# Value products of an attention round issued one round later, in four chained layers on one core

## The reference

```
L0  x = latent attention over (ctx, x), then RMS norm, MLP 512 -> 2048 -> 512 with gelu, residual
L1  x = grouped-query attention of x over ctx (32 query heads, 8 key heads, mask added), layer norm
L2  x = cross attention of layernorm(x) over ctx (16 heads), residual, layer norm, MLP, residual
L3  x = latent attention over (ctx, x), norm, MLP, residual (as L0, other weights)
attention: softmax(scale * Q K^T + mask) V, then an output product with its bias
```

## Time and profile before

| what | value |
|---|---|
| median of 3 runs | 2698.76 us (2697.95 to 2700.19) |
| profiled execution, its own time | 2698.54 us |
| its span (first to last instruction) | 2696.8 us |
| PE / PEld / DVE busy | 2478.5 / 2080.7 / 1284.3 us |
| ACT / POOL busy | 1090.2 / 1104.4 us |
| mean granted TensorE clock | 0.966 |

### The profile page before, as it was taken

The page is one execution under the profiler, slowest core; times in us unless marked ns, Lnnn a source line. Parts: engine busy times, 40 slices in busy tenths (PEclk is TensorE's granted clock), DMA queues, the critical chain, the costliest instruction groups (busy, mean ns, idle before and its releaser), DMA issues.

```text
span 2696.8 us, 47930 instructions
## 1 busy us (share of the span) xinstructions
PE 2478.5 (92%) x18464; PEld 2080.7 (77%) x18464; DVE 1284.3 (48%) x2527; ACT 1090.2 (40%) x3705; POOL 1104.4 (41%) x1972
## 2 busy tenths in 40 slices
PE   7999998999997777758888899999899999899999
PEld 6887886888886666647777788888788888688887
DVE  4556554323226878764445533322355555432322
ACT  4555553111117777755555411111355555311111
POOL 2444446400135888973454570003345444540000
PEclk9999999999998999879989899999999999899999
DMA  4112213111122222221232241101211211321100
GB/s 154 56 56 89 70 36 106 62 45 47 59 74 70 78 91 77 66 69 61 84 103 89 73 125 48 47 34 61 83 48 48 87 48 34 105 63 47 48 32 16
DMA packets 110321, 181.25 MB, mean 67 GB/s; under 512 B 7889, under 2 KB 43409, under 8 KB 109073
## 3 DMA queue, kind: packets, MB, share of 16 engines
q1 hardware_dynamic: 110096, 178.19, 20.2%
HBM read 132.02 MB, written 46.14 MB: 66 GB/s over the span
## 4 chain that ended last, share of the span: by engine, by line
PE 78%; DVE 8%; ACT 5%; POOL 5%; issue 3%; DMA 1%; SPq 0%; DVEq 0%; POOLq 0%; ACTq 0%
PE banks L317 70%; PE banks L453 4%; ACT plain_high L697 3%; PE banks L480 3%; POOL plain_high L1268 2%; DVE neg_max L948 2%; DVE plain_high L944 2%; PE banks L504 1%; DVE plain_work L953 1%; DVE rounded_work L1046 1%; DVE rounded_work L1020 0%; DVE stats L1072 0%; DMA plain_work<-mlp_w 0%; POOL rounded_high L308 0%; PE banks L442 0%
## 5 line engine op out<-in xcount | busy, mean ns | idle before, releaser
L317 PE MATMUL banks<-rounded_work,rounded_low 128*128 128x512 f32 (+1 forms) x2688 | 533.1, 356 | 57.9 <-issue 35.3
L1268 POOL TENSOR_SCALAR plain_high<-plain_high,inv_sum 128x128 f32<-128x128 f32 (+1 forms) x1024 | 388.1, 402 | 407.7 <-DVE inv_sum L966 407.2
L317 PEld LDWEIGHTS banks<-rounded_work,rounded_low 128*128 128x128 f32 x2688 | 445.7, 200 | 124.7 <-issue 53.8
L317 PE MATMUL banks<-rounded_work,rounded_high 128*128 128x512 f32 (+1 forms) x2400 | 488.2, 358 | 8.7 <-DMA rounded_work<-ctx_split 6.2
L925 ACT ACTIVATE plain_work<-banks,columns 128x512 f32<-128x512 f32 x192 | 132.5, 690 | 865.3 <-PE banks L317 865.3
L317 PEld LDWEIGHTS banks<-rounded_work,rounded_high 128*128 128x128 f32 x2400 | 399.7, 193 | 76.4 <-issue 9.8
L1244 DVE CAST rounded_work<-plain_work 128x512 fp32r<-128x512 f32 x192 | 101.3, 528 | 693.7 <-ACT plain_work L925 682.8
L317 PE MATMUL banks<-rounded_low,rounded_work 128*128 128x512 f32 x1728 | 413.1, 391 | 0.0
L317 PE MATMUL banks<-rounded_high,rounded_work 128*128 128x512 f32 (+1 forms) x1728 | 392.8, 380 | 0.0
L317 PEld LDWEIGHTS banks<-rounded_low,rounded_work 128*128 128x128 f32 x1728 | 322.3, 188 | 68.8 <-issue 3.0
L317 PEld LDWEIGHTS banks<-rounded_high,rounded_work 128*128 128x128 f32 x1728 | 311.8, 190 | 60.4 <-issue 1.4
(11 more groups left out here) (101 smaller groups left out, 3063.4 us busy)
## 6 DMA issues: line engine op xcount, KB each, us to landing
plain_work<-x SPq DMA_DIRECT2D x96, 256.0 KB, 2.9
plain_work<-mlp_w SPq DMA_DIRECT2D x96, 256.0 KB, 2.7
rounded_work<-ctx_split SPq DMA_DIRECT2D x24, 1024.0 KB, 6.0
u<-plain_work SPq DMA_DIRECT2D x48, 256.0 KB, 2.8
plain_work<-u SPq DMA_DIRECT2D x12, 1024.0 KB, 6.7
x<-plain_work SPq DMA_DIRECT2D x48, 256.0 KB, 2.1
plain_work<-attention_w SPq DMA_DIRECT2D x44, 256.0 KB, 2.7
plain_work<-inputs_t SPq DMA_DIRECT2D x8, 1024.0 KB, 8.1
```

The costliest lines, as they stand in the source:

```text
L317: mm = pe.matmul(dst, lhs(i), rhs(j), start=first and n == 0, stop=last and n == 2, skip_group_check=True)
L1268: last = pool.tensor_scalar(part, part, inv_sum[:, R % 2, r, g:g + 1], 1.0, ALU.mult, ALU.mult)
```

## The change

The value product of round n moves behind the scores of round n+2 and ahead of the turning of round n+1, on TensorE. On ScalarE its split (`act_heads`) moves to just before the copy of row 0 of round n+1. On VectorE its split (`dve_heads`) moves into `dve_round`, behind the maxima of rows 0 and 1. The last round of a pair crosses into the next pair, and the last one of a layer stands alone after the loop. Of the diff, the latent layer on TensorE, the same in the cross layer, the helper and its use:

```
@@ pe_latent
                 pe_scores(pe, y, p, 1)
+                if p:
+                    pe_attend(pe, y, p - 1, 3)
                 pe_turn_probs(pe, y, p, 0)
...
-                pe_attend(pe, y, p, 0)
                 if more:
                     pe_keys(pe, y, p + 1, 0)
                     pe_keys(pe, y, p + 1, 1)
                 pe_scores(pe, y, p, 2)
+                pe_attend(pe, y, p, 0)
                 pe_turn_probs(pe, y, p, 1)
...
-                pe_attend(pe, y, p, 1)
...
                 pe_scores(pe, y, p, 3)
+                pe_attend(pe, y, p, 1)
                 pe_turn_probs(pe, y, p, 2)
...
-                pe_attend(pe, y, p, 2)
                 if more:
                     pe_keys(pe, y, p + 1, 3)
                     pe_scores(pe, y, p + 1, 0)
+                pe_attend(pe, y, p, 2)
                 pe_turn_probs(pe, y, p, 3)
                 pe_out(pe, y, 2 * p)
-                pe_attend(pe, y, p, 3)
...
+            pe_attend(pe, y, PAIRS - 1, 3)
             pe_out(pe, y, B - 1)
@@ pe_cross
                 pe_scores(pe, y, p, 1)
+                if p:
+                    pe_attend(pe, y, p - 1, 1)
                 pe_turn_probs(pe, y, p, 0)
                 if more:
                     pe_turn_x(pe, y, p + 1)
-                pe_attend(pe, y, p, 0)
...
                 if more:
                     pe_scores(pe, y, p + 1, 0)
+                pe_attend(pe, y, p, 0)
                 pe_turn_probs(pe, y, p, 1)
                 pe_out(pe, y, 2 * p)
-                pe_attend(pe, y, p, 1)
@@ act_cross (act_latent and act_gqa alike, with 3 for 1)
+                if p:
+                    act_heads(act, y, p - 1, 1)
                 act_round(act, y, p, 1, (p, 0), inputs)
-                act_heads(act, y, p, 0)
...
+                act_heads(act, y, p, 0)
                 act_round(act, y, p + 1, 0 if more else None, (p, 1), nothing)
-                act_heads(act, y, p, 1)
@@ dve_round
-        def dve_round(dve, y, p, k, turned, between):
+        def dve_round(dve, y, p, k, turned, between, past=None):
             if k is not None:
                 dve_max(dve, y, p, k, 0)
                 dve_max(dve, y, p, k, 1)
+            if past:
+                dve_heads(dve, y, *past)
             if turned:
                 dve_probs(dve, y, *turned, 1)
@@ dve_cross (dve_latent and dve_gqa alike)
-                dve_round(dve, y, p, 1, (p, 0), inputs)
-                dve_heads(dve, y, p, 0)
+                dve_round(dve, y, p, 1, (p, 0), inputs, (p - 1, 1) if p else None)
...
-                dve_round(dve, y, p + 1, 0 if more else None, (p, 1), nothing)
+                dve_round(dve, y, p + 1, 0 if more else None, (p, 1), nothing, (p, 0))
                 dve_out(dve, y, 2 * p)
-                dve_heads(dve, y, p, 1)
```

More of the change, by code:

```diff
@@ L1128, in dve_latent @@
                     dve_keys(dve, y, p + 1, 1)
-                dve_round(dve, y, p, 2, (p, 1), nothing)
+                dve_round(dve, y, p, 2, (p, 1), nothing, (p, 0))
                 if more:
@@ L1138, in dve_latent @@
                     dve_values(dve, y, p + 1, 1)
-                dve_round(dve, y, p, 3, (p, 2), nothing)
+                dve_round(dve, y, p, 3, (p, 2), nothing, (p, 1))
                 if more:
@@ L1144, in dve_latent @@
                     dve_turn_u(dve, M[y.n], 0, 3)
-                dve_heads(dve, y, p, 2)
                 if more:
                     dve_keys(dve, y, p + 1, 3)
-                dve_round(dve, y, p + 1, 0 if more else None, (p, 3), nothing)
+                dve_round(dve, y, p + 1, 0 if more else None, (p, 3), nothing, (p, 2))
                 dve_out(dve, y, 2 * p)
-                dve_heads(dve, y, p, 3)
                 if more:
                     dve_queries(dve, y, p + 1, 1)
+            dve_heads(dve, y, PAIRS - 1, 3)
             dve_out(dve, y, B - 1)
@@ L1223, in dve_cross @@
                     dve_out(dve, y, 2 * p - 1)
-                dve_round(dve, y, p + 1, 0 if more else None, (p, 1), nothing)
+                dve_round(dve, y, p + 1, 0 if more else None, (p, 1), nothing, (p, 0))
                 dve_out(dve, y, 2 * p)
-                dve_heads(dve, y, p, 1)
+            dve_heads(dve, y, PAIRS - 1, 1)
             dve_out(dve, y, B - 1)
```

56 lines of the change are left out of this document (32 added, 24 removed).

## The result

The moved order is slower: 2733.4 us median (2727.35 to 2737.85) beside 2698.36 (2692.72 to 2700.19) for the kernel before on the same chip, ratio 1.0134 with a 95% interval of 1.0117 to 1.0151, or +35 us. The forecast was +22.7 (2721), the range reached to 2744. The profiled execution of after took 2737.85 us with a span of 2736.0, so the two profiled spans differ by 39.2 us.

The account below looks back on a forecast made before the run. TensorE was taken as nearly full in L3 and L0, with idle time in the cross and grouped-query layers. Terms 7.4 + 2.1 + 10.5 + 7.7 + 1.0 - 6 = +22.7 us on 2698.54 gave 2721, range 2697 to 2744.

Parts of the forecast that it names:

- Cross layer, first and second round: Cross layer: keys 1.75 us later in six pairs (+10.5), row 3 of the second turning waits 1.1 in seven (+7.7).
- the shift: L0, first round: softmax and input split 1.06 us later, keys' wait 1.27 becomes 2.33, seven pairs: +7.4 us.
- rival C: L0: longer waits before the keys lower the clock there too, 22 us more, 2743; chance 0.14.
- one of the signs that I had named for being wrong: Three signs: grouped-query pair under 43 us, latent first copy less than 0.5 us later, or L0 clock below 1.00.
- 1.6 us of a pair: Grouped-query layer: 1.9 less 0.3 us off a pair's 47.45, -11 us over seven pairs, half taken off for the clock.
- waits for GpSimd take the place of those before the value product: Grouped-query layer: waits before the value product vanish, waits for POOL replace them, a pair at 46 to 47 us.
- the ring of four banks: Row 3 of the turning needs the value product's bank, free after VectorE's heads split: +7.7 us cross layer, 0 in L3.
- 0: L3 apart from its last pair: the 1.06 us shift is hidden by TensorE's own work, 0 us.
- Last pairs and the MLP's first rows: Last pairs, where TensorE waits for DMA of the MLP's rows: +1.1 us each in L0 and L3; cross layer +1.0.
- rival A: Grouped-query layer runs free once VectorE stops waiting for the value product: 5 us a pair (-35), 2692; chance 0.11.
- B: L0 and cross layer: only places change, the later softmax is swallowed and the ring does not bind: 2698.5; chance 0.09.
- the 6 us that the grouped-query layer was to give back: Grouped-query layer: scores no longer wait for the value product, net -6 us after half is taken off for the clock.

Follow-up runs that it names:

- e5_after_wide: e4_fix with each round's heads split in the grouped-query and cross layers as one instruction per engine, other biases left out: 2715.35 us, 1.0054 of before.
- e2_cross: The kernel before with the change in the cross layer alone: 2716.42 us, 1.0050 of before.
- e4_fix: The changed kernel with VectorE's last heads split of the grouped-query layer moved ahead of block 14's second moments: 2725.20 us, 1.0088 of before.
- e1_gqa: The kernel before with the change in the grouped-query layer alone, VectorE's last heads split ahead of block 14's second moments: 2699.24 us, 0.9988 of before.
- e7_gqa_norm: e1_gqa with one normalising instruction of GpSimd per row instead of four, three sums left out: 2690.27 us, 0.9967 of before.
- e8_before_ring: The kernel before with three of VectorE's four moments blocks a pair in the grouped-query layer moved ahead of the reciprocals: 2726.91 us, 1.0088 of before.
- e3_latent: The kernel before with the change in L0 and L3 alone: 2710.68 us, 1.0029 of before.
- e11_gqa_ring: e1_gqa with three of VectorE's moments blocks a pair moved ahead of the round's reciprocals: 2708.13 us, 1.0026 of before.
- e9_latent_early: e3_latent with L0's split of the next pair's inputs one step earlier on ScalarE and VectorE: 2696.83 us, 0.9979 of before.

## Why the prediction held, and where it didn't

**Cross layer, first and second round: right, mechanism and size.** +18.2 forecast, +16.0 measured, with the two waits at 5.09 and 0.96 us: the first round came out at 1.49 us a pair (1.75 forecast), the second at 0.96 (1.1). e5_after_wide takes away the split's length and with it 1.3 of the 2.3 us a pair. In after the second pair takes 45.42 us, with matmuls at a granted clock of 0.50 behind its wait of 5.80 us (1260 to 1265 us); in e2_cross and e4_fix it takes 42.07 and 42.44 after 5.57 and 5.56 us, so this part belongs to one execution.

**L0: the shift was right, the clock was not in the sum.** The copy starts 1.71 us after the step that stands first, where it was 0.70: 1.01 later (1.06 forecast). The wait of six pairs' keys grew by 0.85, and the keys of pair 1 start 0.40 us later (55.57 for 55.17): 5.5 of the 7.4. Two of six pairs pay 1.6 us more for the clock. That is rival C, in part: 3.2 us of its 22, and one of the signs that I had named for being wrong, a clock below 1.00 in L0, came (0.99). The two lines at 109.86 and 161.81 have the same wait, and the burst of matmuls behind it was fast in one pair and slow in the other.
The Trainium skill (TensorE: Matmul & The Clock Gate, "HAM oscillation — how this bites in real kernels") tells of a kernel in which the burst behind every wait starts at the low clock; the slow pair agrees with that, the fast one doesn't.

**Grouped-query layer: the step "1.6 us of a pair" failed.** Five pairs, from the third to the last input turning, give 47.06 us each in before and 46.92 in e1_gqa. I had written that waits for GpSimd take the place of those before the value product; it was the heads' split (42.6 us), and the waits for GpSimd fell from 19.9 to 16.9. I had used the ring of four banks for the cross layer and L3, not here, where the value product's bank is also the one that row 3 of the turning takes. Two cuts at single links gave little: neither a shorter split (e5_after_wide, 0.33 us) nor less normalising (e7_gqa_norm, 0.19) moved the mean of six pairs by much, though the last pair of e7_gqa_norm is 3 us shorter. What the pair's 47 us are made of stays open, with two accounts left. By one, exponentials, reciprocals, normalising, sums and maxima follow one another over four engines and hold the pair at its length whatever TensorE waits for; e8_before_ring shows of it only that late reciprocals lengthen the pair. By the other, the gain came and the clock took it: 1.2 us more of matmuls a pair at 0.87 for 0.91, beside the 1.6 us that the pair was to lose, of which the prediction had taken off half. No run has the new order in this layer at the old clock, so the runs don't tell the two apart.

**The end of the grouped-query layer: missing from the sum.** The edit moved VectorE's last heads' split behind the moments of block 14, which wait for GpSimd. The prediction counted the last pairs of the other layers (+1 each) and left this one at nothing: 5.7 us of wait, 8.4 us with the clock, and e4_fix gives them back. It is the largest single miss that an experiment gives back.

**L3: "0" was about right, in part by luck.** The profiles give +2.0 in after, +1.2 in e3_latent and -1.6 in e4_fix. In e3_latent 0.27 us is gained in each of five pairs and 2.5 are lost in the second, whose keys wait 2.83 us for the input split and then run slow. The prediction had looked for L3's new wait at the ring, where none came, and not at these keys.

**Last pairs and the MLP's first rows.** In L0 +1.1 forecast, +0.9 measured: from the last keys with such a wait to the first matmul of the MLP 60.96 us for 60.03 (433.85 less 372.89, and 424.10 less 364.07). Behind the cross layer +1.0 forecast, 2 to 3 us measured where it repeats, 6.7 in the profile of after. In L3 +1.1 forecast and none came: the rest of the kernel is 0.3 to 0.5 us shorter in after, e3_latent and e4_fix.

Against rival A: no pair of the grouped-query layer in after fell under 45.9 us. Against B: the computed waits came. The sum was 12 us short of the medians. Three terms are more than that (some 14 to 17 us), and the cross layer, 2 us below its forecast, gives a part back: the end of the grouped-query layer, priced at nothing; the clock in L0, likewise; and the 6 us that the grouped-query layer was to give back, of which 1.0 came. That the time still lies within the range is partly luck: the range was wide for the sake of rival C, and most of what it had to take in was none of the rivals.

## What to carry to other kernels

When a step moves in an order written by hand, go through each engine's list and ask at every new place what the instruction now stands *behind*, above all in the last round, where the surrounding work differs: one split behind one moment block cost as much as L0's seven shifts. A wait in front of a step is worth what is late next: here 45.6 us of waiting vanished, 42.6 us of another took its place, the matmuls ran at a lower clock, and the pair did not change. A move that loses by itself can be what makes another one pay: the earlier input split costs 0.7% in the old order (1.0073) and gains 0.5% in the new one (1.0029 to 0.9979), because the value product had left the place that the split delays.

## What the runs showed of the hardware

The same wait of 2.12 us before the same 24 matmuls was followed by 5.74 us of them in one pair and 7.35 in the next, in turn for four pairs and then not again (51.96, 53.56, 51.95, 53.6, 51.95, 51.95). In e3_latent, e4_fix and e5_after_wide two of the six pairs were slow as well, not always the same two. Between the second and the last input turning of the grouped-query layer the mean granted clock was 0.87 with the value products moved and 0.90 to 0.92 without; with less normalising (e7_gqa_norm) or the moments moved (e8_before_ring, e11_gqa_ring) it was 0.84 to 0.85. Waits of 1.27 us (before) and 0.72 us (e9_latent_early) once a pair left all pairs at the higher clock. Splits of 4 x 128 columns in one instruction instead of four took TensorE's row-3 waits of 0.96 us in the cross layer to nothing. In before they were worth 0.12% (interval 0.9979 to 0.9998).
